# Parametric relu on ScalarE, and the mask added to the logits in PSUM by VectorE, in a two-layer graph attention kernel

## The chip, the cores and the metric

The program runs on one core of one Trainium2 chip. The metric is the device time of one execution in microseconds (us). The kernel before has a median of 1155.83 us over 3 runs (1154.28 to 1158.36).

## The reference

The input is x, 64 graphs of 128 nodes with 384 features, and adj, a boolean 128x128 matrix for each graph. Two layers follow each other, each with a residual and a layer norm:

```
# layer 0: six heads of 64
q, k, v = heads(x @ Wq + bq), heads(x @ Wk + bk), heads(x @ Wv + bv)
probs = softmax(q @ k.T / 8 + where(adj, 0, -9e15))
x1 = layernorm(x + (probs @ v) @ Wf + bf)

# layer 1: twelve heads of 32
h = x1 @ W1                       # per head
th = tanh(h)
attn = (th @ w_src) + (th @ w_dst).T
attn = where(attn >= 0, attn, 0.2 * attn)
attn = where(adj, attn, -999)
f = elu(softmax(attn) @ h + b1)
gate = sigmoid(x1 @ Hw.T + Hb)
out = layernorm(x1 + gate * f + (1 - gate) * x1)
```

## The kernel before, in words

All 64 graphs go through one software pipeline that is written out in full; every engine has its own list of instructions, and semaphores order them. The outer loop runs over groups g of four graphs, the inner loop over j = 0 to 3. In one iteration the kernel works on three graphs at once. TensorE also projects q, k and v of the next group (lines 267 to 322: in the iterations j = 0, 1 and 2 two projections with 512 columns each, in j = 3 the four projections of v). Graph ta = 4(g-1)+j is in its first layer's attention ("att" in the code). Graph tl = ta-2 is in the first half of the second layer ("gat"). The second layer's softmax, product and normalisation of tl-1 and tl-2 are the "tail". In the last group (graphs 60 to 63) there are no projections left, and after it two iterations have no first layer.

The order inside an iteration is fixed on each engine. On TensorE (lines 485 to 534): scores of ta, turn_f of tl-2, turn_x1 of tl, the first projection (fill_a), project_h, the second projection (fill_b), turn_p0, then the gate's product, the turns of the previous graph's weights (turn_p1), context and project_out in pieces, turn_sd, logits, the next scores' mask, apply_p1.

The second layer's logits are a sum of a row value and a column value for each head. Three bf16 parts of both lie in `sd3`; turn_sd transposes them into `ps_t` (a part of bank `ps_c`); ScalarE copies the row half into `rows_L` in three instructions (line 675), VectorE expands the column half into `cols_R` (line 891). A matmul of `rows_L` and `cols_R` then makes four heads' logits in one bank of `ps_d`; there are three banks, q = 0, 1, 2. Before it a matmul of a scaled identity (`ident_100`, 2^100) with `mask` (0 or -1, bf16) puts -2^100 where there is no edge (line 448). The leaky relu is made in two steps: ScalarE evicts Relu(0.8 x) to `z` (line 684), and VectorE computes z = 0.2 x + z (line 917). The next iteration takes the maxima of z (lines 805 and 813).

VectorE's order in the part touched is: `cols_R`; for the tail two graphs behind the second sum `r1` and its statistics (lines 897 to 901); the first layer's sum `r0` and its statistics (lines 908 to 912); the three steps of line 917. Then the next iteration begins with the maxima of the first layer's scores (line 783). ScalarE's first exponentials (line 615) wait for these, and `inv0` (line 811) for the exponentials.

GpSimd (lines 974 to 1012) takes, in each iteration: `p0` times `inv0` (line 982, which turn_p0 on TensorE waits for), `thw` (line 990), every now and then an addition for the residual or a split of x, then `normalise` for `r1` (it waits for `mv1_ready`, the end of line 901), and after that `normalise` for `r0` (it waits for `mv0_ready`, the end of line 912). Each `normalise` is four instructions (lines 967 to 972).

The first layer's mask comes from `ident_53` (2^53) times the same `mask`, in `scores_mask`.

Of the kernel before, what the change touches and what calls it, by code (L numbers as in the profile page):

```python
# [48 lines left out]
def build_program(nc, xT_in, x, adj, Wq, bq, Wk, bk, Wv, bv, Wf, bf, W1, b1, w_src, w_dst, HwT, Hb,  # L49
                  ident_in, pick_in, out):  # L50
    with ExitStack() as ctx:
        def sb(name, shape, dt=F32):
            return ctx.enter_context(nc.sbuf_tensor(name, shape, dt))
# [80 lines left out]
        def staging(buffer):  # L134
# [16 lines left out]
            sd_ready split_small sd3_ready sd_turned rows_ready cols_ready logits_ready relu_ready z_ready neg1_ready  # L151
# [34 lines left out]
        def has_tail(n, j, lag=1):  # L186
            return 0 <= G * (n - 1) + j - LAG - lag < B
# [62 lines left out]
        def _(pe):  # L250
# [84 lines left out]
            def scores_mask(t):  # L335

                if due(t):
                    pe.wait_ge(S["p0T_even"], t)
                    pe.wait_ge(S["p0T_odd"], t)
                if t % (B // 4) == 0:  # L340
                    pe.wait_ge(S["mask_ready"], t // (B // 4) + 1)
                if t == 0:
                    pe.wait_ge(S["consts_ready"], 3)
                    pe.wait_ge(S["bf_ready"], 1)
                for o in range(2):
                    pe.matmul(ps_s[:, o, 0:C * N].rearrange("p (i n) -> p i n", i=C), ident_53[:],  # L346
                              mask[:, t, :].unsqueeze(1).broadcast_to([P, C, N]), start=True, stop=False)

            def scores(g, par, j):
# [89 lines left out]
            def logits(t):  # L439

                pe.wait_ge(S["h_ready"], t + 1)
                pe.wait_ge(S["gate_ready"], t + 1)
                m = mask[:, t, :].unsqueeze(1) if isinstance(t, int) else mask[:, bass.ds(t, 1), :]
                for q in range(3):
                    if due(t):
                        pe.wait_ge(S[f"p1T_{q}"], t)
                    heads = ps_d[:, q, :].rearrange("p (a n) -> p a n", a=4)
                    pe.matmul(heads, ident_100[:], m.broadcast_to([P, 4, N]), start=True, stop=False)  # L448
                    if q == 0:
                        pe.wait_ge(S["rows_ready"], t + 1)  # L450
                        pe.wait_ge(S["cols_ready"], t + 1)
                    last = pe.matmul(heads, rows_L[:, q, :], cols_R[:], start=False, stop=True)  # L452
                    last.then_inc(S["logits_ready"], 1)

            def turn_p1(t, next_is_here, groups):
# [82 lines left out]
        def _(act):  # L538
# [25 lines left out]
            def iteration(g, par, n):  # L564
# [36 lines left out]
                for j in range(G):  # L601
# [68 lines left out]
                    if gat:  # L670
                        act.wait_ge(S["sd_turned"], tl + 1)
                        if due(tl):
                            act.wait_ge(S["logits_ready"], 3 * tl)
                        for q in range(3):
                            last = act.activation(rows_L[0:64, q, :], ps_t[0:64, :], ACT.Copy, scale=of_bank[0:64, q:q + 1])  # L675
                        last.then_inc(S["rows_ready"], 1)
                    if tail:
                        turned_p1(tl - 1, 2)
                    if gat:
                        for q in range(3):  # L680
                            act.wait_ge(S["logits_ready"], 3 * tl + q + 1)
                            if due(tl):
                                act.wait_ge(S["p1_turned"], 3 * (tl - 1) + q + 1)
                            act.activation(z[:, 4 * q:4 * q + 4, :], ps_d[:, q, :].rearrange("p (a n) -> p a n", a=4),  # L684
                                           ACT.Relu, scale=0.8).then_inc(S["relu_ready"], 1)
                    if tail:
                        act.wait_ge(S["ph_made"], tl)
                        if due(tl - 1):
# [7 lines left out]
        def _(dve):  # L696
# [19 lines left out]
            def small_constants():  # L716

                dve.wait_ge(S["ident_in_ready"], 16)
                dve.tensor_copy(ident_b[:], ident[:]).then_inc(S["consts_ready"], 1)
                dve.tensor_scalar(ident_53[:], ident[:], 2.0 ** 53, None, ALU.mult).then_inc(S["consts_ready"], 1)  # L720
                dve.tensor_scalar(ident_100[:], ident[:], 2.0 ** 100, None, ALU.mult).then_inc(S["consts_ready"], 1)
# [22 lines left out]
            def iteration(g, par, n):  # L744
# [29 lines left out]
                for j in range(G):  # L774
# [112 lines left out]
                    if gat:  # L887
                        dve.wait_ge(S["sd_turned"], tl + 1)
                        if due(tl):
# [1 line left out]
                        dve.tensor_tensor(cols_R[64:P, :, :], ps_t[64:P, :].unsqueeze(1).broadcast_to([64, 4, N]),  # L891
                                          of_slot[64:P, :].unsqueeze(2).broadcast_to([64, 4, N]), ALU.mult
                                          ).then_inc(S["cols_ready"], 1)
                    if has_tail(n, j, 2):
                        t2 = tl - 2
                        dve.wait_ge(S["tail_small"], 3 * t2 + 3)
                        dve.scalar_tensor_tensor(r1[:], r1[:], 0.25, x1_, ALU.mult, ALU.add).then_inc(S["r1_ready"], 1)
                        dve.wait_ge(S["r1_ready"], t2 + 1)
                        dve.bn_stats(st1, r1[:]).then_inc(S["mv1_ready"], 1)
                        dve.wait_ge(S["mv1_ready"], apart(dve, 2 * t2 + 1))  # L900
                        dve.bn_aggr(mv1, st1).then_inc(S["mv1_ready"], 1)  # L901
# [11 lines left out]
                    if gat:  # L913

                        for q in range(3):
                            dve.wait_ge(S["relu_ready"], 3 * tl + q + 1)
                            dve.scalar_tensor_tensor(z[:, 4 * q:4 * q + 4, :],  # L917
                                                     ps_d[:, q, :].rearrange("p (a n) -> p a n", a=4), 0.2,
                                                     z[:, 4 * q:4 * q + 4, :], ALU.mult, ALU.add
                                                     ).then_inc(S["z_ready"], 1)  # L920
            pipeline(dve, iteration)


        @block_.gpsimd
        def _(pool):
# [129 lines left out]
```

## Time and profile before

| | |
|---|---|
| median of 3 runs | 1155.83 us (1154.28 to 1158.36) |
| profiled execution, its own time | 1157.4 us |
| its span, first to last instruction | 1155.6 us |
| mean granted TensorE clock | 0.987 of full speed |
| TensorE matmul busy | 1093.0 us, 95% |
| VectorE busy | 989.8 us, 86% |
| ScalarE busy | 920.0 us, 80% |
| GpSimd busy | 544.0 us, 47% |

In the rows PE is TensorE's matmuls, PEld its weight loads, DVE VectorE, ACT ScalarE, POOL GpSimd, SP SyncE. L12 is line 12 of the kernel. Names such as `out<-in` are the program's buffers without their numbers. Matmuls overlap, so their busy time is more than the time between the starts. A busy share is an average over the whole span: it does not tell which engine another waits for.

### The profile page before, as it was taken

What the parts mean: (1) busy time and instruction counts of PE and PEld (TensorE: products, weight loads), DVE (VectorE), ACT (ScalarE), POOL (GpSimd) and SP (SyncE); (2) the same over time, 40 slices, a digit from 0 to 9 for tenths busy, and PEclk for the clock granted to TensorE, in tenths of its full rate; (3) what the DMA queues carried; (4) which work ended last, traced back from release to release, by engine and by line L of the source; (5) the groups of instructions that cost most, each with busy time, mean ns of one, the idle gap of its engine ahead of it and who ended that gap; (6) DMA issues with size and microseconds to landing.
All of it is one profiled execution on the core that took longest, in us unless ns stands there. A gap on an engine that the chain in (4) does not pass through costs nothing.

```text
span 1155.6 us, 25654 instructions
## 1 busy us (share of the span) xinstructions
PE 1093.0 (95%) x8364; PEld 900.8 (78%) x8428; DVE 989.8 (86%) x2022; ACT 920.0 (80%) x3383; POOL 544.0 (47%) x717
## 2 busy tenths in 40 slices
PE   5889999999999999999999999999999999997773
PEld 5668888888888888888888888888888888885652
DVE  5447989899898989889898998989898898989986
ACT  3338888888888888888888888888888888888875
POOL 0454544544454454445445444544544454444332
PEclk9989999999999999999999999999999999999997
DMA  9101010020101002010100101010010101000000
GB/s 264 55 2 55 16 48 34 10 70 16 62 15 52 32 9 69 16 62 15 52 31 9 70 15 63 16 51 34 8 69 15 63 15 43 15 8 15 15 14 21
DMA packets 25894, 44.67 MB, mean 39 GB/s; under 512 B 2462, under 2 KB 23714, under 8 KB 25762
## 3 DMA queue, kind: packets, MB, share of 16 engines
q1 hardware_dynamic: 23234, 41.91, 10.5%
q10 hardware_dynamic: 2496, 1.12, 0.5%
q8 instruction: 69, 1.13, 0.4%
q14 instruction: 63, 0.52, 0.1%
q0 software_dynamic: 32, 0.00, 0.0%
HBM read 30.43 MB, written 12.58 MB: 37 GB/s over the span
## 4 chain that ended last, share of the span: by engine, by line
PE 90%; DVE 3%; POOL 2%; issue 2%; ACT 2%; DMA 1%; POOLq 0%; ACTq 0%; DVEq 0%
PE ps_b L255 22%; PE ps_d L255 18%; PE ps_a L255 13%; PE ps_d L464 7%; PE ps_a L384 5%; PE ps_s L356 4%; PE ps_d L448 4%; PE ps_c L474 4%; PE ps_s L364 4%; PE ps_c L482 2%; PE ps_d L452 2%; PE ps_s L346 2%; PE ps_b L411 2%; ACT z L588 1%; PE ps_d L431 1%
## 5 line engine op out<-in xcount | busy, mean ns | idle before, releaser
L588 ACT ACTIVATE z<-z,s 128x128 f32<-128x128 f32 x768 | 299.2, 404 | 0.5 <-DVE s L805 0.5
L967 POOL TENSOR_SCALAR s<-s 128x1 f32<-128x1 f32 x128 | 28.6, 223 | 354.5 <-DVE s L901 325.7
L982 POOL TENSOR_TENSOR p<-p,s 128x768 f32<-128x768 f32 x64 | 94.2, 1472 | 181.2 <-DVE s L811 181.2
L615 ACT ACTIVATE p<-ps_s,s 128x128 f32<-128x128 f32 x384 | 135.4, 372 | 49.3 <-DVE s L783 49.3
L588 ACT ACTIVATION_READ_ACCUMULATOR z<-z,s 128x1 f32 x768 | 156.4, 204 | 0.0
L464 PE MATMUL ps_d<-ident,z 128*128 128x128 f32 x768 | 118.4, 277 | 9.4 <-ACT z L588 8.4
L990 POOL TENSOR_TENSOR thw<-th,w_sd 128x768 f32<-128x768 f32 x64 | 117.8, 1840 | 6.8 <-ACT th L638 6.8
L917 DVE SCALAR_TENSOR_TENSOR z<-ps_d,z 128x512 f32<-128x512 f32 x192 | 118.7, 674 | 0.9 <-ACT z L684 0.9
L684 ACT ACTIVATE z<-ps_d 128x512 f32<-128x512 f32 x192 | 100.8, 597 | 4.4 <-remote 0.5
L464 PEld LDWEIGHTS ps_d<-ident,z 128*128 128x128 f32 x768 | 90.6, 142 | 17.4 <-ACT z L588 9.2
L606 ACT ACTIVATE x1T_hi<-ps_b 128x384 fp32r<-128x384 f32 x64 | 31.6, 493 | 78.1 <-PE ps_b L411 78.1
L255 PE MATMUL ps_d<-hw_hi,x1T_hi 128*128 128x384 f32 x192 | 82.3, 429 | 0.0
L255 PE MATMUL ps_b<-wf_hi,ctxT_hi 128*128 128x384 f32 x192 | 79.2, 413 | 2.7 <-DVE ctxT_lo L749 1.3
L615 ACT ACTIVATION_READ_ACCUMULATOR p<-ps_s,s 128x1 f32 x384 | 80.6, 210 | 0.0
L448 PE MATMUL ps_d<-mask,ident 128*128 128x512 bf16 x192 | 73.5, 383 | 4.5 <-ACT rows_L L675 1.3
L805 DVE TENSOR_REDUCE s<-z 128x8 f32<-128x1024 f32 x64 | 77.3, 1208 | 0.0
L970 POOL TENSOR_TENSOR s<-s,minus_half 128x1 f32<-128x1 f32 x128 | 72.2, 564 | 10.7
L598 ACT ACTIVATE p1T<-ps_d 128x512 f32<-128x512 f32 x128 | 75.2, 588 | 0.7 <-PE ps_d L464 0.7
L836 DVE COPY p0T<-ps_s 128x384 f32<-128x384 f32 x64 | 35.7, 558 | 44.4 <-PE ps_s L364 44.2
L255 PE MATMUL ps_d<-w_hi,x1T_hi 128*128 128x384 f32 x192 | 65.2, 340 | 8.9 <-DVE x1T_lo L749 8.9
L255 PE MATMUL ps_b<-wf_lo,ctxT_hi 128*128 128x384 f32 x192 | 65.4, 340 | 0.0
L255 PE MATMUL ps_d<-hw_lo,x1T_hi 128*128 128x384 f32 x192 | 65.0, 338 | 0.0
(158 smaller groups left out, 3492.2 us busy)
## 6 DMA issues: line engine op xcount, KB each, us to landing
x_cols<-in_xT_dram SPq DMA_DIRECT2D x16, 768.0 KB, 6.2
xb<-in_x_dram SPq DMA_DIRECT2D x16, 768.0 KB, 4.7
out_dram<-y SPq DMA_DIRECT2D x64, 192.0 KB, 1.8
z<-in_L_gnn_Wq_dram SPq DMA_DIRECT2D x1, 576.0 KB, 7.0
p1T<-in_L_gnn_Wk_dram SPq DMA_DIRECT2D x1, 576.0 KB, 9.0
qT<-in_L_gnn_Wv_dram SPq DMA_DIRECT2D x1, 576.0 KB, 11.6
kT<-in_L_gnn_Wf_dram SPq DMA_DIRECT2D x1, 576.0 KB, 13.8
z<-in_L_gnn_W_dram SPq DMA_DIRECT2D x1, 576.0 KB, 11.5
```

The costliest lines, as they stand in the source:

```text
L255: last = pe.matmul(out_ap, lhs(a, c), rhs(b, c), start=(c == 0 and k == 0), stop=(closed and c == C - 1 and k == 2))
L448: pe.matmul(heads, ident_100[:], m.broadcast_to([P, 4, N]), start=True, stop=False)
L464: last = pe.transpose(ps_d[:, q, (a % 4) * N:(a % 4 + 1) * N], z[:, a, :], ident[:])
L588: done = act.activation(z[:, a, :], z[:, a, :], ACT.Exp, bias=neg1[:, a:a + 1], accum_out=sum1[:, a:a + 1])
L598: act.activation(p1T[:, 4 * q:4 * q + 4, :], ps_d[:, q, :].rearrange("p (a n) -> p a n", a=4), ACT.Copy).then_inc(S[f"p1T_{q}"], 1)
L615: last = act.activation(p0[:, o, i, :], ps_s[:, o, i * N:(i + 1) * N], ACT.Exp, bias=neg0[:, k:k + 1], accum_out=sum0[:, k:k + 1])
L684: act.activation(z[:, 4 * q:4 * q + 4, :], ps_d[:, q, :].rearrange("p (a n) -> p a n", a=4), ACT.Relu, scale=0.8).then_inc(S["relu_ready"], 1)
L805: dve.tensor_reduce(neg1[:, 0:8], z[:, 0:8, :], AX_X, ALU.max, negate=True).then_inc(S["neg1_ready"], 1)
L917: dve.scalar_tensor_tensor(z[:, 4 * q:4 * q + 4, :], ps_d[:, q, :].rearrange("p (a n) -> p a n", a=4), 0.2, z[:, 4 * q:4 * q + 4, :], ALU. ...
L970: pool.tensor_tensor(rs, ve, minus_half[:], ALU.pow).then_inc(S[small], 1)
L982: pool.tensor_tensor(p0[:].rearrange("p o i n -> p (o i) n"), p0[:].rearrange("p o i n -> p (o i) n"), inv0.unsqueeze(2).broadcast_to([P, ...
L990: pool.tensor_tensor(thw[:], th[:].unsqueeze(1).broadcast_to([P, 2, D]), w_sd[:], ALU.mult).then_inc(S["thw_ready"], 1)
```

## The change

The mask is scaled once, on GpSimd, to 0 or -2^53. The first layer adds it with the plain identity. In the second layer TensorE no longer adds it: the logits' matmul stands alone, and VectorE adds the mask to the bank in PSUM, in three instructions that stand directly behind `cols_R`. ScalarE then evicts the bank with a parametric relu (slope 0.2) straight to the finished `z`; VectorE's three steps of line 917 are gone. On VectorE the order behind the three additions is now: `r0` and its statistics, then `r1` and its statistics. GpSimd's order is as it was. `rows_ready` is counted once for each of the three copies instead of once for all.

```diff
@@ TensorE
-                    pe.matmul(ps_s[...], ident_53[:],
+                    pe.matmul(ps_s[...], ident_b[:],
                               mask[:, t, :]..., start=True, stop=False)
@@ logits
+                pe.wait_ge(S["cols_ready"], t + 1)
                 for q in range(3):
+                    pe.wait_ge(S["rows_ready"], 3 * t + q + 1)
                     if due(t):
                         pe.wait_ge(S[f"p1T_{q}"], t)
-                    pe.matmul(heads, ident_100[:], m.broadcast_to([P, 4, N]), start=True, stop=False)
-                    if q == 0:
-                        pe.wait_ge(S["rows_ready"], t + 1)
-                        pe.wait_ge(S["cols_ready"], t + 1)
-                    last = pe.matmul(heads, rows_L[:, q, :], cols_R[:], start=False, stop=True)
+                    last = pe.matmul(heads, rows_L[:, q, :], cols_R[:], start=True, stop=True)
                     last.then_inc(S["logits_ready"], 1)
@@ ScalarE
-                        last.then_inc(S["rows_ready"], 1)      # once for the three copies; now behind each
...
-                            act.wait_ge(S["logits_ready"], 3 * tl + q + 1)
+                            act.wait_ge(S["masked_ready"], 3 * tl + q + 1)
-                                           ACT.Relu, scale=0.8).then_inc(S["relu_ready"], 1)
+                                           ACT.Prelu, alpha=0.2).then_inc(S["z_ready"], 1)
@@ VectorE, constants
-                dve.tensor_scalar(ident_53[:], ident[:], 2.0 ** 53, None, ALU.mult)...
-                dve.tensor_scalar(ident_100[:], ident[:], 2.0 ** 100, None, ALU.mult)...
@@ VectorE, behind cols_R
-                    if has_tail(n, j, 2):          # r1 and its statistics: moved to the end
+                    if gat:
+                        for q in range(3):
+                            heads = ps_d[:, q, :].rearrange("p (a n) -> p a n", a=4)
+                            if tl % (B // 4) == 0:
+                                dve.wait_ge(S["mask_ready"], tl // (B // 4) + 1)
+                            dve.wait_ge(S["logits_ready"], 3 * tl + q + 1)
+                            dve.tensor_tensor(heads, heads, mask[:, tl, :]..., ALU.add
+                                              ).then_inc(S["masked_ready"], 1)
                     if att:                        # r0 and its statistics, as before
...
-                            dve.wait_ge(S["relu_ready"], 3 * tl + q + 1)
-                            dve.scalar_tensor_tensor(z[...], ps_d[...], 0.2, z[...], ALU.mult, ALU.add
-                                                     ).then_inc(S["z_ready"], 1)
+                    if has_tail(n, j, 2):          # r1 and its statistics, unchanged in themselves
@@ GpSimd
-                pool.tensor_scalar(mask[...], adj_u8[...], 1.0, -1.0, ALU.mult, ALU.add
+                pool.tensor_scalar(mask[...], adj_u8[...], 2.0 ** 53, -(2.0 ** 53), ALU.mult, ALU.add
```

## Rows read from the trace of the kernel before

**Rows 1.** The page, parts 1 and 4: busy time; shares of the last chain.
```profile
PE 1093.0 (95%) x8364; PEld 900.8 (78%) x8428; DVE 989.8 (86%) x2022; ACT 920.0 (80%) x3383; POOL 544.0 (47%) x717
...
PE 90%; DVE 3%; POOL 2%; issue 2%; ACT 2%; DMA 1%; POOLq 0%; ACTq 0%; DVEq 0%
```

**Rows 2.** Busy by stretch: from:to, length, PE, PEld, DVE, ACT, POOL, clock, DMA.
```profile
601.27:617.51 16.24, 16.19 (x128) 13.27 (x128) 15.07 (x31) 13.83 (x53) 8.40 (x11) 1.00 0.04 13
617.51:636.30 18.79, 18.65 (x147) 16.12 (x147) 15.48 (x32) 15.62 (x57) 10.21 (x12) 1.00 0.04 12
636.30:652.41 16.11, 16.06 (x127) 13.10 (x127) 15.06 (x31) 13.74 (x53) 6.62 (x10) 1.00 0.32 111
...
1088.03:1103.90 15.87, 12.51 (x110) 9.86 (x110) 14.35 (x31) 13.24 (x53) 6.61 (x10) 1.00 0.04 13
1103.90:1155.60 51.70, 27.53 (x212) 18.62 (x213) 37.20 (x75) 31.74 (x112) 13.68 (x26) 0.81 0.05 20
```

**Rows 3.** Waits over the span: who, for whom, us, times, longest.
```profile
POOL s L967 <- DVE s L901: 325.7, 64, 7.1
POOL p L982 <- DVE s L811: 181.2, 62, 4.3
```

**Rows 4.** Timeline of PE: start, us, what, idle before.
```profile
602.05 0.82 PE L448 MATMUL ps_d<-mask,ident 128*128 128x512 bf16 x2
602.71 0.38 PE L452 MATMUL ps_d<-cols_R,rows_L 128*128 128x512 bf16 x1
...
605.44 0.55 PE L482 MATMUL ps_c<-ident,fT 128*128 128x128 f32 x3
...
611.90 0.82 PE L364 MATMUL ps_s<-ident,p 128*128 128x128 f32 x6
...
624.21 0.41 PE L255 MATMUL ps_b<-wv_hi,xT_hi 128*128 128x384 f32 x1
```

**Rows 5.** Timeline of DVE.
```profile
601.27 0.69 DVE L891 TENSOR_TENSOR cols_R<-ps_c,choose 64x512 bf16<-64x512 bf16 x1 [0.15 <-PE ps_c L437]
602.00 0.56 DVE L897 SCALAR_TENSOR_TENSOR r<-r,x 128x384 f32<-128x384 f32 x1
...
603.40 0.56 DVE L908 TENSOR_TENSOR r<-ps_b,xb 128x384 f32<-128x384 f32 x1
...
604.69 1.85 DVE L917 SCALAR_TENSOR_TENSOR z<-ps_d,z 128x512 f32<-128x512 f32 x3
606.46 0.95 DVE L783 TENSOR_REDUCE s<-ps_s 128x6 f32<-128x768 f32 x1
...
623.56 0.55 DVE L749 TENSOR_TENSOR x1T_lo<-ps_b,x1T_hi 128x384 fp32r<-128x384 f32 x1
...
668.65 0.69 DVE L891 TENSOR_TENSOR cols_R<-ps_c,choose 64x512 bf16<-64x512 bf16 x1 [0.15 <-PE ps_c L437]
```

**Rows 6.** Timeline of POOL, the last row from the last group.
```profile
603.46 0.23 POOL L967 TENSOR_SCALAR s<-s 128x1 f32<-128x1 f32 x1 [4.63 <-DVE s L901]
...
606.76 0.67 POOL L972 TENSOR_SCALAR x<-r,s 128x384 f32<-128x384 f32 x1
609.96 1.47 POOL L982 TENSOR_TENSOR p<-p,s 128x768 f32<-128x768 f32 x1 [2.53 <-DVE s L811]
...
1096.71 1.47 POOL L982 TENSOR_TENSOR p<-p,s 128x768 f32<-128x768 f32 x1 [2.53 <-DVE s L811]
```

**Rows 7.** Timeline of ACT.
```profile
602.69 1.57 ACT L684 ACTIVATE z<-ps_d 128x512 f32<-128x512 f32 x3
604.70 0.49 ACT L690 ACTIVATE fT<-ps_c 128x384 f32<-128x384 f32 x1 [0.44 <-PE ps_c L474]
```

**Rows 8.** Groups by line, whole span: busy us, mean ns, idle before.
```profile
L917 DVE SCALAR_TENSOR_TENSOR z<-ps_d,z 128x512 f32<-128x512 f32 x192 | 118.7, 674 | 0.9 <-ACT z L684 0.9
...
L795 DVE TENSOR_TENSOR ps_c<-ps_c,s 128x384 f32<-128x384 f32 x64 | 36.2, 566 | 6.3 <-PE ps_c L482 4.2
...
L545 ACT ACT_TABLE_LOAD x1 | 1.3, 1283 | 0.9 <-issue 0.9
```

More of the change, by code:

```diff
@@ L70, in build_program @@
         ident_b = sb("ident_b", [P, P], BF16)
-        ident_53 = sb("ident_53", [P, P], BF16)
-        ident_100 = sb("ident_100", [P, P], BF16)
         choose = sb("choose", [P, 7])
@@ L150, in build_program @@
             x1_turned x1_hi x1_lo h_made h_ready th_ready gate_made gate_ready thw_ready
-            sd_ready split_small sd3_ready sd_turned rows_ready cols_ready logits_ready relu_ready z_ready neg1_ready
+            sd_ready split_small sd3_ready sd_turned rows_ready cols_ready logits_ready masked_ready z_ready neg1_ready
             exp1_ready p1_turned p1T_0 p1T_1 p1T_2 ph_made fT_ready f_turned inv1_ready f_ready minus_one_ready b1_ready
@@ L342, in scores_mask @@
                 if t == 0:
-                    pe.wait_ge(S["consts_ready"], 3)
+                    pe.wait_ge(S["consts_ready"], 1)
                     pe.wait_ge(S["bf_ready"], 1)
                 for o in range(2):
-                    pe.matmul(ps_s[:, o, 0:C * N].rearrange("p (i n) -> p i n", i=C), ident_53[:],
+                    pe.matmul(ps_s[:, o, 0:C * N].rearrange("p (i n) -> p i n", i=C), ident_b[:],
                               mask[:, t, :].unsqueeze(1).broadcast_to([P, C, N]), start=True, stop=False)
@@ L442, in logits @@
                 pe.wait_ge(S["gate_ready"], t + 1)
-                m = mask[:, t, :].unsqueeze(1) if isinstance(t, int) else mask[:, bass.ds(t, 1), :]
+                pe.wait_ge(S["cols_ready"], t + 1)
                 for q in range(3):
+                    pe.wait_ge(S["rows_ready"], 3 * t + q + 1)
                     if due(t):
@@ L674, in iteration @@
                         for q in range(3):
-                            last = act.activation(rows_L[0:64, q, :], ps_t[0:64, :], ACT.Copy, scale=of_bank[0:64, q:q + 1])
-                        last.then_inc(S["rows_ready"], 1)
+                            act.activation(rows_L[0:64, q, :], ps_t[0:64, :], ACT.Copy, scale=of_bank[0:64, q:q + 1]
+                                           ).then_inc(S["rows_ready"], 1)
                     if tail:
@@ L719, in small_constants @@
                 dve.tensor_copy(ident_b[:], ident[:]).then_inc(S["consts_ready"], 1)
-                dve.tensor_scalar(ident_53[:], ident[:], 2.0 ** 53, None, ALU.mult).then_inc(S["consts_ready"], 1)
-                dve.tensor_scalar(ident_100[:], ident[:], 2.0 ** 100, None, ALU.mult).then_inc(S["consts_ready"], 1)
                 dve.wait_ge(S["const_in"], 16 * 7)
@@ L893, in iteration @@
                                           ).then_inc(S["cols_ready"], 1)
-                    if has_tail(n, j, 2):
[L895 to L901, printed above, removed]
+                    if gat:
[4 more added lines that the diff above has]
+                            dve.wait_ge(S["logits_ready"], 3 * tl + q + 1)
+                            dve.tensor_tensor(heads, heads, mask[:, tl, :].unsqueeze(1).broadcast_to([P, 4, N]), ALU.add
+                                              ).then_inc(S["masked_ready"], 1)
                     if att:
@@ L912, in iteration @@
                         dve.bn_aggr(mv0, st0).then_inc(S["mv0_ready"], 1)
-                    if gat:
-                        for q in range(3):
-                            dve.wait_ge(S["relu_ready"], 3 * tl + q + 1)
-                            dve.scalar_tensor_tensor(z[:, 4 * q:4 * q + 4, :],
-                                                     ps_d[:, q, :].rearrange("p (a n) -> p a n", a=4), 0.2,
-                                                     z[:, 4 * q:4 * q + 4, :], ALU.mult, ALU.add
-                                                     ).then_inc(S["z_ready"], 1)
+                    if has_tail(n, j, 2):
+                        t2 = tl - 2
+                        dve.wait_ge(S["tail_small"], 3 * t2 + 3)
+                        dve.scalar_tensor_tensor(r1[:], r1[:], 0.25, x1_, ALU.mult, ALU.add).then_inc(S["r1_ready"], 1)
+                        dve.wait_ge(S["r1_ready"], t2 + 1)
+                        dve.bn_stats(st1, r1[:]).then_inc(S["mv1_ready"], 1)
+                        dve.wait_ge(S["mv1_ready"], apart(dve, 2 * t2 + 1))
+                        dve.bn_aggr(mv1, st1).then_inc(S["mv1_ready"], 1)
             pipeline(dve, iteration)
@@ L942, in mask_quarter @@
                 pool.wait_ge(S["adj_in"], 16)
-                pool.tensor_scalar(mask[:, quarter, :], adj_u8[:, quarter, :], 1.0, -1.0, ALU.mult, ALU.add
+                pool.tensor_scalar(mask[:, quarter, :], adj_u8[:, quarter, :], 2.0 ** 53, -(2.0 ** 53), ALU.mult, ALU.add
                                    ).then_inc(S["mask_ready"], 1)
```

## The prediction

> **What bounds the kernel now.** I read the page first. TensorE is busy for 95% of the span and holds 90% of the chain that ended last; VectorE has 86%, GpSimd 47% [rows 1]. By this page TensorE is the bound, and a change that takes matmuls from it should pay. The second view was the stretches, cut at the starts of `cols_R` (L891), since the changed work stands right behind it. An iteration takes 16.24 us (j = 2, and j = 1 is the same within 0.01), 18.79 us (j = 3) or 16.11 us (j = 0) [rows 2]. A group of four takes 668.65 - 601.27 = 67.38 us [rows 5]. In these stretches TensorE has no idle time to speak of. But the row 1088.03:1103.90 speaks against the page. It is from the last group, where TensorE has no projections left and is busy for 12.51 us only, and the iteration still takes 15.87 us [rows 2]. So there is a second loop, only 0.24 to 0.37 us shorter than TensorE's. Taking more than that from TensorE brings nothing in j = 0, 1, 2, and whatever lengthens the second loop by more than that shows in the time.
>
> The second loop is found with the waits and the timelines. GpSimd waits 181.2 us in 62 waits for `inv0` (L811) [rows 3]. In the last group `p0` times `inv0` (L982) starts 1096.71 - 1088.03 = 8.68 us behind `cols_R`, and the next `cols_R` follows 1103.90 - 1096.71 = 7.19 us later [rows 2, 6]. In the full stretch it starts 609.96 - 601.27 = 8.69 us behind, the same, and ends at 611.43; TensorE comes to turn_p0 at 611.90, 0.47 us later [rows 4 to 6]. So the loop is: `cols_R`, the rest of VectorE's list, the maxima (L783), ScalarE's six exponentials, `inv0`, `p0` on GpSimd, turn_p0, and from there work that the change leaves alone up to the next `cols_R`.
>
> The other wait of GpSimd, 325.7 us for L901 [rows 3], looks harmless, since it is idle time of an idle engine. It tells that GpSimd takes `r1` first, in program order, and that its two normalisations are set off by the end of VectorE's `r1`. They run from 603.46 to 606.76 + 0.67 = 607.43, 3.97 us together, and leave 2.53 us before `inv0` comes [rows 6].
>
> **The change part by part.** Times below are counted from the start of `cols_R` (601.27).
>
> TensorE: three mask matmuls go. From 602.05 to 602.71 it issues three of these 512-column matmuls, 0.22 us each [rows 4], so 0.66 us an iteration. As a matmul with the same columns, the first layer's mask costs what it did, since only its constant changes.
>
> VectorE, the work: three steps of L917 go (674 ns, three of them advance VectorE from 604.69 to 606.46, 1.77 us) [rows 5, 8], and three additions of the same 512 columns come, PSUM to PSUM with a bf16 operand. The trace has no such instruction at this size. Its nearest rows are L917 from below (674 ns) and, from above, L795, in place in PSUM with 384 columns (566 ns), to which 128 columns at about 1.05 ns make some 700 ns [rows 8]. The additions are thus worth 0 to 0.1 us more in sum; I take 0, so 1.77 us.
>
> VectorE, the new wait: the first addition needs the first bank's logits, which need `cols_R`. `cols_R` ends at +0.69, TensorE is free for the logits at 602.05, +0.78, and such a matmul takes 0.38 us [rows 4, 5]; with a hand-over the addition starts at +1.20. Before, VectorE went on at 602.00, +0.73, with `r1` [rows 5]. So 0.47 us of idle time is new. Bounds: 0.35 if the matmul is seen sooner, 0.6 if TensorE has to wake up for it. Queued behind it on VectorE are `r0`, `r1` and the maxima L783. The third bank's matmul also waits for ScalarE's last copy of p1T, just ahead of 602.69, and is there before the third addition at about +2.4.
>
> VectorE, the new order: additions +1.20 to +2.97; the `r0` part as between 603.40 and 604.69, 1.29 us, to +4.26; the `r1` part as between 602.00 and 603.40, 1.40 us, to +5.66; then L783. It started at 606.46, +5.19, before [rows 5]. L783 is 0.47 us late.
>
> GpSimd: this is where the order bites. It starts on `r1` 603.46 - 602.00 = 1.46 us after VectorE's first `r1` instruction [rows 5, 6], now at 4.26 + 1.46 = +5.72 instead of +2.19. Both normalisations need 3.97 us, so GpSimd is free at +9.7; with a gap between two of its instructions I take +9.75. `inv0`, 0.47 us late, would have let `p0` start at 8.69 + 0.47 = +9.16. So `p0` starts at +9.75, 1.06 us late, and 0.59 us of that is GpSimd's queue. Bounds: 9.65 and 9.95.
>
> From `p0` to the next `cols_R` it is 7.19 us, measured in the group where TensorE has idle time [rows 2, 6]. The new iteration is 9.75 + 7.19 = 16.94 us: +0.70 against 16.24, +0.83 against 16.11, +1.07 in the last group against 15.87. TensorE's 0.66 us are gone into waiting for `p0`.
>
> In j = 3 TensorE has over 2 us more of projections and GpSimd's queue is covered: `p0` has over a microsecond of room there. But project_v(1) at 624.21 waits for x1T_lo, which follows L783 on VectorE (623.56 + 0.55 = 624.11) [rows 4, 5]. It is 0.47 us late, and behind it TensorE is busy without a gap up to turn_p0. So j = 3 costs +0.47. The 0.66 us saved ahead of it do not help, because turn_f (605.44) now waits for `fT`.
>
> ScalarE: the count of instructions stays. A Prelu of the same tile with immediate scale is put at Relu's 597 ns; three take 1.57 us from first start to last end [rows 7]. They follow the additions: the third ends near +3.07, its Prelu near +3.7, `fT` (0.49 us) near +4.15; TensorE can start turn_f at about +4.2. It starts at 605.44, +4.17, now [rows 4, 7]. No loss, no gain.
>
> Start and end: two small constants less on VectorE, worth 0.3 us at most, and one late L749 after graph 63, 0.5 us. Both together +0.2. `rows_ready` counted singly is hidden by `cols_R`, which the first logits wait for anyway. No DMA is touched.
>
> **The sum.** `r1` exists from graph 4 on, so the new order reaches `p0` of graphs 5 to 63. Groups of graphs 4 to 59, 14 of them: 0.83 + 0.70 + 0.70 + 0.47 = 2.70 us each, 37.8, less 0.8 for graph 4. Last group: 4 x 1.07 = 4.3. With 0.2 for start and end: +41.5 us. The profiled execution, 1157.4 us with a span of 1155.6, would take 1198.9. It lay 1.6 us above the median 1155.83, so I say 1197.5 us, 3.6% slower. With the bounds of `p0`'s start (9.65 to 9.95) and of the additions the sum is +34 to +55.
>
> **A page's rule against the price of Prelu.** The trace has one ACT_TABLE_LOAD, of 1283 ns, for all of Copy, Identity, Exp, Tanh and Relu [rows 8]. The Trainium skill, page "ScalarE: Activation LUTs", section "Table sets: the hidden batching unit", says that cheap functions are filler in every set and names relu, copy, identity and abs, but not the parametric relu; a function of another set is preceded by a load. It puts a switch, drain included, at about 2.66 us; by that, two switches in each of 64 iterations would be an estimated 340 us and the time about 1540.
>
> **The rivals.**
> A. GpSimd's queue does not bind, because its normalisations run closer together or `inv0` comes later than I think. Then only VectorE's wait counts: `p0` at +9.16, the iteration 16.35 us, +0.11, +0.11, +0.24 and +0.47 in a group, 14 x 0.93 + 4 x 0.48 = 15 us: 1171. For it: the 2.53 us of idle time before L982 [rows 6]. Against it: L967 moves by 3.53 us, more than that room and the 0.47 us together (3.00).
> B. The other side: TensorE is the bound, as the page says, and VectorE catches up. Then the saving is limited by the last group's loop: 0.37 + 0.37 + 0.24 in j = 1, 2, 0 and 0.66 in j = 3, 1.64 us in a group, 15 groups: -25 us, 1131. It decides if `p0` starts at or before 16.24 - 7.19 = +9.05, so if the additions wait for nothing and GpSimd is not held. For it: 90% of the last chain is PE [rows 1]. Against it: every step of the walk.
> C. Prelu isn't in the table in use. Two loads of 1283 ns in each of 64 iterations, 164 us if nothing covers them; ScalarE waits 0.44 us before `fT` [rows 7] and for the maxima, so perhaps half is seen: 1280, from 1230 to 1360.
> D. The granted clock falls, since TensorE gets idle time. Against it: it is 1.00 in the last group with TensorE busy for 12.51 of 15.87 us, and 0.81 only in the drained end [rows 2]. No case of its own.
>
> **How the numbers follow.** Forecast 0.82 (1189 to 1210), A 0.07, B 0.04, C 0.04, and 0.03 for a wash of unknown parts near 1156. A measurement of this kernel can tell 0.3%, some 3.5 us, from no change. Faster 0.04, the same 0.03, slower 0.93. The range runs from 1174, towards A, to 1210, the upper bounds.
>
> **What would show it.** In the changed trace: `cols_R` to `cols_R` about 16.9 us in j = 0, 1, 2 and 19.3 in j = 3, and the last group also 16.9, no longer shorter than the rest. Idle time of about 0.5 us on VectorE ahead of the first addition. L982 no longer waiting 2.5 us for VectorE but starting right behind L972. TensorE idle for `p0` ahead of L364 by over 1 us in most iterations. Additions of 670 to 700 ns, Prelu near 600 ns, one table load. I am wrong if L982 still waits for `inv0`, or if iterations of j = 0, 1, 2 are under 16.3 us.

## The result and the profile after

The changed kernel takes 1210.51 us (median of 4 runs, 1208.89 to 1211.59), the kernel before, in the same sessions, 1157.09. The ratio is 1.046, with a 95% interval of 1.0444 to 1.0477. The forecast was 1197.5 us, 3.6% slower: the sign and the two mechanisms (VectorE's new wait and GpSimd's queue) were right, and the time lies 0.5 us above the range. The rise is 53.4 us where about 42 was forecast, so a fifth of it was missed; 1.3 us of the distance to 1197.5 is only the starting point, which was the earlier median of 1155.83. The profiled execution has a span of 1209.8 us, 54.2 us more than before.

First the page of the changed kernel, parts 1 and 4. TensorE's share of the last chain has gone from 90% to 52%, GpSimd's from 2% to 19%, VectorE's from 3% to 21% [rows 1].

```profile
PE 1103.7 (91%) x8236; PEld 882.5 (73%) x8236; DVE 989.7 (82%) x2020; ACT 927.3 (77%) x3383; POOL 542.4 (45%) x717
...
PE 52%; DVE 21%; POOL 19%; issue 6%; ACT 2%; DMA 0%; POOLq 0%; ACTq 0%; DVEq 0%
```

The stretches, cut at the starts of `cols_R` as in [rows 2]: a j = 1 iteration, j = 3, j = 0, one of the last group, one of the drained end (the two iterations that follow it and have no first layer).

```profile
608.70:625.78 17.08, 16.42 (x126) 12.81 (x125) 15.06 (x31) 13.93 (x53) 8.37 (x11) 1.00 0.04 13
642.87:662.33 19.46, 18.41 (x145) 15.84 (x144) 15.47 (x32) 15.71 (x57) 10.22 (x12) 1.00 0.04 12
662.33:679.44 17.11, 16.24 (x125) 12.68 (x124) 15.06 (x32) 13.86 (x54) 6.58 (x10) 1.00 0.31 105
1120.58:1137.67 17.09, 13.51 (x108) 10.63 (x107) 14.34 (x30) 13.39 (x52) 6.57 (x10) 0.90 0.04 13
1169.17:1185.12 15.95, 10.24 (x63) 7.72 (x61) 11.36 (x24) 9.57 (x36) 3.49 (x5) 0.81 0.04 14
```

Every iteration but j = 3 now takes 17.1 us, with TensorE's projections or without. That is what a bound away from TensorE looks like. (j = 2, 625.78 to 642.87, takes 17.09 us.) The first four of these rows show the iterations that the sum was about; the last one matters for the size of the miss.

The waits of the changed kernel. GpSimd waited for `inv0` 62 times before [rows 3]; now it does 17 times, in j = 3 and at the start. In the others it comes late to an `inv0` that is already there, and TensorE waits for it.

```profile
POOL s L960 <- DVE s L913: 542.7, 64, 10.9
...
DVE ps_d L893 <- PE ps_d L447: 41.3, 64, 1.3
...
PEld ps_s L362 <- POOL p L975: 36.6, 46, 2.0
...
POOL p L975 <- DVE s L804: 19.1, 17, 1.6
```

The timeline of VectorE from one `cols_R` (591.60) to the next (608.70): the wait for the logits, the three additions, r0, r1, the maxima.

```profile
591.60 0.69 DVE L884 TENSOR_TENSOR cols_R<-ps_c,choose 64x512 bf16<-64x512 bf16 x1
592.92 1.90 DVE L893 TENSOR_TENSOR ps_d<-ps_d,mask 128x512 f32<-128x512 f32 x3 [0.63 <-PE ps_d L447]
594.84 0.56 DVE L901 TENSOR_TENSOR r<-ps_b,xb 128x384 f32<-128x384 f32 x1
...
596.13 0.53 DVE L909 SCALAR_TENSOR_TENSOR r<-r,x 128x384 f32<-128x384 f32 x1
...
597.38 0.94 DVE L776 TENSOR_REDUCE s<-ps_s 128x6 f32<-128x768 f32 x1
...
608.70 0.69 DVE L884 TENSOR_TENSOR cols_R<-ps_c,choose 64x512 bf16<-64x512 bf16 x1 [0.16 <-PE ps_c L435]
```

The timeline of GpSimd in the same iteration. `p0` (L975) follows r0's normalisation without a gap, where 2.53 us of idle time stood [rows 6].

```profile
597.55 0.23 POOL L960 TENSOR_SCALAR s<-s 128x1 f32<-128x1 f32 x1 [7.48 <-DVE s L913]
...
600.86 0.67 POOL L965 TENSOR_SCALAR x<-r,s 128x384 f32<-128x384 f32 x1
601.49 1.48 POOL L975 TENSOR_TENSOR p<-p,s 128x768 f32<-128x768 f32 x1
```

The timeline of TensorE there: the logits, turn_f waiting for `fT`, the first of project_h, turn_p0 waiting for `p0`. The wait for `p0` is short here (0.27 us), because TensorE has already lost time at the logits, at `fT` and at x1T_lo; in the last group, from which the last row is, it is 1.07 us.

```profile
592.50 0.88 PE L447 MATMUL ps_d<-cols_R,rows_L 128*128 128x512 bf16 x3
...
595.88 0.55 PE L477 MATMUL ps_c<-ident,fT 128*128 128x128 f32 x3 [0.51 <-ACT fT L685]
...
598.84 0.44 PE L253 MATMUL ps_d<-w_hi,x1T_hi 128*128 128x384 f32 x1
...
603.02 0.88 PE L362 MATMUL ps_s<-ident,p 128*128 128x128 f32 x6 [0.27 <-POOL p L975]
...
1132.00 0.87 PE L362 MATMUL ps_s<-ident,p 128*128 128x128 f32 x6 [1.07 <-POOL p L975]
```

The groups of the changed instructions: the addition, Prelu, the one table load.

```profile
L893 DVE TENSOR_TENSOR ps_d<-ps_d,mask 128x512 f32<-128x512 f32 x192 | 121.3, 693 | 41.3 <-PE ps_d L447 41.3
...
L679 ACT ACTIVATE z<-ps_d 128x512 f32<-128x512 f32 x192 | 114.6, 598 | 47.6 <-DVE ps_d L893 47.5
...
L540 ACT ACT_TABLE_LOAD x1 | 1.3, 1283 | 1.0 <-issue 1.0
```

### The profile page after: what moved, and what is told of

The parts are those of the page before. It is cut to its first block, busy times and chain, and to the rows that moved or that the text cites. A ratio compares the mean times of both kernels' runs of the same rounds, so it can differ in the third digit from the quotient of the medians.

```text
span 1209.8 us, 25470 instructions
## 1 busy us (share of the span) xinstructions
PE 1103.7 (91%) x8236; PEld 882.5 (73%) x8236; DVE 989.7 (82%) x2020; ACT 927.3 (77%) x3383; POOL 542.4 (45%) x717
## 4 chain that ended last, share of the span: by engine, by line
PE 52%; DVE 21%; POOL 19%; issue 6%; ACT 2%; DMA 0%; POOLq 0%; ACTq 0%; DVEq 0%
PE ps_b L253 14%; PE ps_d L253 12%; DVE ps_d L893 10%; PE ps_d L459 7%; PE ps_a L253 5%; POOL p L975 5%; POOL s L963 4%; PE ps_s L362 4%; PE ps_a L382 4%; POOL x L965 3%; POOL y L965 3%; DVE r L901 2%; DVE s L911 2%; DVE s L903 2%; PE ps_d L447 2%
## 5 line engine op out<-in xcount | busy, mean ns | idle before, releaser
L893 DVE TENSOR_TENSOR ps_d<-ps_d,mask 128x512 f32<-128x512 f32 x192 | 121.3, 693 | 41.3 <-PE ps_d L447 41.3
L679 ACT ACTIVATE z<-ps_d 128x512 f32<-128x512 f32 x192 | 114.6, 598 | 47.6 <-DVE ps_d L893 47.5
L975 POOL TENSOR_TENSOR p<-p,s 128x768 f32<-128x768 f32 x64 | 94.3, 1473 | 19.1 <-DVE s L804 19.1
L253 PE MATMUL ps_d<-w_hi,x1T_hi 128*128 128x384 f32 x192 | 71.9, 374 | 11.0 <-DVE x1T_lo L742 10.7
L362 PE MATMUL ps_s<-ident,p 128*128 128x128 f32 x384 | 54.9, 279 | 16.2 <-POOL p L975 16.2
L362 PEld LDWEIGHTS ps_s<-ident,p 128*128 128x128 f32 x384 | 42.2, 140 | 37.5 <-POOL p L975 36.6
L253 PE MATMUL ps_d<-w_hi,x1T_lo 128*128 128x384 f32 x192 | 67.3, 350 | 0.0
```

Of the source, the lines that this page charges most:

```text
L253: last = pe.matmul(out_ap, lhs(a, c), rhs(b, c), start=(c == 0 and k == 0), stop=(closed and c == C - 1 and k == 2))
L362: last = pe.transpose(ps_s[:, o, i * N:(i + 1) * N], p0[:, o, i, :], ident[:])
L893: dve.tensor_tensor(heads, heads, mask[:, tl, :].unsqueeze(1).broadcast_to([P, 4, N]), ALU.add).then_inc(S["masked_ready"], 1)
L975: pool.tensor_tensor(p0[:].rearrange("p o i n -> p (o i) n"), p0[:].rearrange("p o i n -> p (o i) n"), inv0.unsqueeze(2).broadcast_to([P, ...
```

## The experiments

"Iteration" below is the time from `cols_R` to `cols_R` in j = 1 and 2 of the full stretch (the iterations in which TensorE projects); offsets count from `cols_R`'s start. The diffs give the order of the lists in words; apart from what they say the instructions are unchanged. Kernels before in the same sessions: 1158.68, 1156.24 and 1157.64 us.

| run | iteration / j = 3, us | median, us | ratio (95%) |
|---|---|---|---|
| before | 16.24 / 18.78 | 1157 | 1 |
| the change | 17.09 / 19.4 | 1210.5 | 1.046 (1.0444 to 1.0477) |
| GpSimd r0 first | 16.64 / 19.4 | 1192.5 | 1.029 (1.0266 to 1.0315) |
| r1 ahead of r0 | 16.90 / 19.4 | 1204.2 | 1.040 (1.038 to 1.0416) |
| GpSimd r0 first, fT early | 16.62 / 19.4 | 1189.7 | 1.028 (1.0247 to 1.0306) |
| wait filled | 16.37 / 18.65 | 1169.8 | 1.011 (1.0079 to 1.0135) |
| wait filled, GpSimd r0 first | 16.35 / 18.65 | 1165.8 | 1.007 (1.005 to 1.0095) |
| the same, fT early | 15.91 / 18.65 | 1145.1 | 0.990 (0.9887 to 0.992) |
| additions last | 20.0 / 22.2 | 1368.2 | 1.183 (1.1799 to 1.1864) |
| before, r1 last | 16.63 / 18.9 | 1177.7 | 1.018 (1.0145 to 1.0208) |
| before, Prelu alone | 16.24 / 18.45 | 1151.1 | 0.994 (0.9917 to 0.9957) |
| two banks by TensorE | 16.03 / 18.23 | 1136.5 | 0.983 (0.9817 to 0.9846) |
| one bank by TensorE | 15.80 / 18.50 | 1135.2 | 0.982 (0.9806 to 0.9836) |
| one bank, two ahead of v | 15.79 / 18.23 | 1128.1 | 0.975 (0.9722 to 0.9779) |

**The order of the sums alone, in the kernel before.**

```diff
-  cols_R; r1 part; r0 part; three steps of the leaky relu
+  cols_R; r0 part; three steps of the leaky relu; r1 part
```

> The kernel before with one thing of the change only: VectorE's r1 part stands last, behind r0 and the three steps of the leaky relu. VectorE has the same work and no new wait. Theory: GpSimd starts at 3.79 + 1.46 = +5.25 instead of +2.19, is free at +9.2, p0 starts there instead of +8.69, the iteration is 9.2 + 7.19 = 16.35 to 16.4 us in j = 0, 1, 2 (16.24, 16.24, 16.11 before) and in the last group (15.87), j = 3 as before: about +8 us, 1165. Rival (the order of the sums costs nothing by itself): 1157 us.

Measured: 1177.7 us, 19 us more than before, with the same work on every engine; 8 us was expected. The mechanism held and its size was larger: r0, now first, waits 0.28 us for TensorE (`out_made`), which I had not counted, and `p0` starts at 617.29 - 607.87 = +9.42, not +9.2. The next `cols_R` follows 7.21 us later. GpSimd in this run:

```profile
613.35 0.23 POOL L967 TENSOR_SCALAR s<-s 128x1 f32<-128x1 f32 x1 [7.62 <-DVE s L920]
...
616.66 0.67 POOL L972 TENSOR_SCALAR x<-r,s 128x384 f32<-128x384 f32 x1
617.29 1.47 POOL L982 TENSOR_TENSOR p<-p,s 128x768 f32<-128x768 f32 x1
```

**GpSimd's order repaired in the changed kernel.**

```diff
-  normalise(r1 ...); normalise(r0 ...)
+  normalise(r0 ...); normalise(r1 ...)
```

> The changed kernel with GpSimd normalising r0 first and r1 second, VectorE as it is. Theory: r0's normalisation can start at +4.6, r1's follows at +6.6 and ends near +8.6, before inv0; p0 waits for inv0 again and starts at +9.3 instead of +9.89, so an iteration of j = 0, 1, 2 takes 16.5 us instead of 17.09, j = 3 stays at 19.4, the last group 16.5; about 1182 us in all. L982's counterpart waits for VectorE's inv0 again in all iterations. Rival (the additions' wait alone): no change, 1210 us.

Measured: 1192.5 us and 16.64 us an iteration. A third of the 53 us was GpSimd's order (in the iterations of j = 1 and 2 it is 0.45 of 0.85 us), since `p0` waits for `inv0` again and starts at 623.59 - 614.32 = +9.27, as expected. But 9.27 + 7.19 would make 16.46. The rest is on TensorE: project_h starts 0.05 us after x1T_lo (620.96 + 0.55 = 621.51 on VectorE), at +7.24 instead of 608.24 - 601.27 = +6.97 in the kernel before, and TensorE is busy from there through turn_p0, which it reaches after `p0` is ready (625.06). The last group gained nothing: `p0` starts at 1111.47 - 1102.20 = +9.27 there too, but the granted clock is 0.90 and the iteration 17.10 us instead of the 16.5 expected. GpSimd's row, VectorE's, TensorE's, and TensorE's in the kernel before:

```profile
623.59 1.47 POOL L975 TENSOR_TENSOR p<-p,s 128x768 f32<-128x768 f32 x1 [0.38 <-DVE s L804]
```
```profile
620.96 0.55 DVE L742 TENSOR_TENSOR x1T_lo<-ps_b,x1T_hi 128x384 fp32r<-128x384 f32 x1
```
```profile
621.56 0.45 PE L253 MATMUL ps_d<-w_hi,x1T_hi 128*128 128x384 f32 x1
...
625.34 0.82 PE L362 MATMUL ps_s<-ident,p 128*128 128x128 f32 x6
```
```profile
608.24 0.33 PE L255 MATMUL ps_d<-w_hi,x1T_hi 128*128 128x384 f32 x1
```

**VectorE's order repaired instead.**

```diff
-  three additions; r0 part; r1 part
+  three additions; r1 part; r0 part
```

> The changed kernel with VectorE's r1 part ahead of the r0 part, both still behind the three additions. Theory (GpSimd's queue is what delays p0): its normalisations start at about +4.7 (first r1 instruction +3.24, plus 1.46) instead of +5.95 and no longer hold p0, which would go at +9.3. But r0 now ends at about +5.2 instead of +3.8, and turn_x1 on TensorE waits for it (it started at +4.66), with 6.1 us of TensorE work from there to turn_p0: so a new wait takes the place of the old one, the iteration is 16.9 to 17.0 us instead of 17.09 and the whole about 1203 us. Rival (only GpSimd's queue counts): 16.5 us an iteration, about 1183 us. Rival (the additions' own work and wait is all, the order of the sums costs nothing): no change, 1210 us.

Measured: 1204.2 us, 16.90. The expectation of a new wait held: turn_x1 on TensorE now waits for r0. Its row:

```profile
627.60 0.55 PE L409 MATMUL ps_b<-ident,x 128*128 128x128 f32 x3 [0.33 <-DVE r L909]
```

**GpSimd r0 first, and `fT` early.** ScalarE takes `fT` behind the first Prelu.

```diff
-  Prelu 0, Prelu 1, Prelu 2, fT
+  Prelu 0, fT, Prelu 1, Prelu 2
```

> The changed kernel with GpSimd normalising r0 first (as in the run before with that alone, 16.64 us) and, besides, ScalarE taking fT behind the first Prelu, so that turn_f on TensorE waits for nothing (it idles 0.4 us there). Theory: nothing is gained, 1192 us and 16.64 us, because project_h still waits for x1T_lo at +7.2, which follows the late maxima on VectorE. Rival (the late fT is what costs 0.4 us an iteration): 16.25 us, 1167.

Measured: 1189.7 us and 16.62 us: the wait for `fT` (0.4 us) is gone and has moved to project_h, as expected.

```profile
620.35 0.44 PE L253 MATMUL ps_d<-w_hi,x1T_hi 128*128 128x384 f32 x1 [0.51 <-DVE x1T_lo L750]
```

**The wait filled.** r1's first instruction stands in VectorE's wait for the logits.

```diff
-  cols_R; three additions; r0 part; r1 part
+  cols_R; r1 sum; three additions; r0 part; r1 statistics
```

> The changed kernel with one thing moved: r1's first instruction stands between cols_R and the three additions, in VectorE's wait for the logits. GpSimd keeps its order. Theory: the maxima come at +5.1 instead of +5.8, GpSimd starts on r1 at +5.25 instead of +5.95, frees p0 at +9.1 to 9.2: 16.3 to 16.4 us an iteration instead of 17.09, j = 3 18.8, about 1165 us. Rival (the additions' work costs, not the wait): less than 0.2 us an iteration gained, over 1200 us.

Measured: 1169.8 us, 16.37. One instruction of 0.56 us moved into the wait takes 41 us off. The maxima start at 608.37 - 603.32 = +5.05 although the additions are all still there. The total is 5 us above the expected one, the iteration as expected. In the last group of the profiled execution two iterations take 16.37 us and two 17.9 us, with the same instructions; the granted clock is 0.81 in the longer ones. VectorE, then two of these iterations:

```profile
608.37 0.94 DVE L776 TENSOR_REDUCE s<-ps_s 128x6 f32<-128x768 f32 x1
```
```profile
1061.49:1079.40 17.91, 14.43 (x107) 11.48 (x107) 14.25 (x31) 13.65 (x53) 6.56 (x10) 0.81 0.03 12
1079.40:1095.77 16.37, 12.06 (x107) 9.54 (x107) 14.24 (x30) 13.36 (x52) 6.57 (x10) 1.00 0.04 14
```

**The wait filled, and GpSimd r0 first.** Both edits together.

```diff
-  cols_R; three additions; r0 part; r1 part            # VectorE
-  normalise(r1 ...); normalise(r0 ...)                 # GpSimd
+  cols_R; r1 sum; three additions; r0 part; r1 statistics
+  normalise(r0 ...); normalise(r1 ...)
```

> As the run with the wait filled alone, and GpSimd normalising r0 first as well. Theory: p0 goes at +8.6 and the iteration is TensorE's again with turn_f 0.1 us later than in the kernel before: 16.35 us, j = 3 18.7, about 1157 us; what is missing against the version that also takes fT early (15.91 us, 1145) is the wait for fT. Rival (GpSimd's queue no longer matters once the wait is filled): the same as the wait filled alone.

Measured: 1165.8 us, 16.35. The iteration is as expected, the total 9 us above. In the full stretch the rival was right: with the wait filled, `p0` behind GpSimd's queue (+9.16, here +8.55) is no later than TensorE with its late turn_f, so repairing the queue brings 0.02 us an iteration. That is 1 us of the 4 us between the two runs. In the profiled executions they differ in the last group and the drained end, where this run has no iteration at a clock of 0.81; how much of the rest is the queue and how much the clock was not separated.

**The same, and `fT` early on ScalarE.**

```diff
-  Prelu 0, Prelu 1, Prelu 2, fT
+  Prelu 0, fT, Prelu 1, Prelu 2
```

> The changed kernel with all three additions on VectorE, and three things moved: r1's first instruction stands between cols_R and the additions (in the wait for the logits), GpSimd normalises r0 first, ScalarE takes fT behind the first Prelu. Theory: L783 at +5.35 instead of +5.78, p0 at +8.85 and no longer behind GpSimd's queue, turn_f not held by fT; iteration 16.05 us in j = 0, 1, 2, 18.95 in j = 3, 16.03 in the last group, about 1155 us: what the change costs is gone, but hardly anything is gained. Rival (the additions cost by themselves, whatever stands where): still over 1185 us.

Measured: 1145.1 us, 15.91; better than expected, since the maxima come at +5.06 and not +5.35. Here the change's whole content is kept and it is 1.0% faster than the kernel before. The rival falls: the three additions by themselves do not cost the loss. VectorE of this run has no idle time between `cols_R` and r0:

```profile
591.79 0.69 DVE L892 TENSOR_TENSOR cols_R<-ps_c,choose 64x512 bf16<-64x512 bf16 x1 [0.16 <-PE ps_c L435]
592.52 0.56 DVE L898 SCALAR_TENSOR_TENSOR r<-r,x 128x384 f32<-128x384 f32 x1
593.11 1.90 DVE L905 TENSOR_TENSOR ps_d<-ps_d,mask 128x512 f32<-128x512 f32 x3
594.92 0.55 DVE L913 TENSOR_TENSOR r<-ps_b,xb 128x384 f32<-128x384 f32 x1
```

**The additions where the old steps stood.**

```diff
-  three additions; r0 part; r1 part
+  r1 part; r0 part; three additions
```

> The changed kernel with VectorE's order as in the kernel before: r1, r0, and the three additions last, where the three steps of the leaky relu stood. Theory: the maxima L783 come at +5.35 (5.19 before), GpSimd is as before, so neither of the two delays of the changed kernel is there; but ScalarE's three Prelus now follow additions that end at +4.2, +4.8 and +5.4, fT starts near +6.0 instead of +3.4, and turn_f stands ahead of turn_x1 and the projections on TensorE: turn_f at +6.5 instead of +4.17, so TensorE loses about 2.3 us an iteration, 18.5 us instead of 16.24, and the whole goes to about 1290 us. Rival (ScalarE has time: it waited 1.15 us ahead of L606): an iteration of 16.3 us, 1160 us.

Measured: 1368.2 us, 20.0 us an iteration. turn_f starts at 750.02 - 743.68 = +6.34, close to the +6.5 expected; 1.5 us an iteration more than the expected 18.5 is there besides. It is the granted clock: 0.91 over the stretch, and behind the idle time of 2.58 us the next 512-column matmuls start 0.43 to 0.57 us apart instead of 0.23. The trace has its own comparison. Five iterations of its full stretch ran at 1.00, and those of j = 0, 1, 2 among them took 18.42 us, with the same wait for `fT`: TensorE idles 2.49 us in both the second and the third row below (j = 1 and j = 2 of one group). The stretch from 743.68, these two, then TensorE in the first:

```profile
743.68:763.41 19.73, 17.06 (x125) 13.99 (x124) 15.11 (x31) 13.95 (x53) 6.65 (x10) 0.91 0.27 91
438.10:458.08 19.98, 17.49 (x126) 14.18 (x125) 15.10 (x31) 14.05 (x53) 8.43 (x11) 0.91 0.03 11
458.08:476.50 18.42, 15.93 (x126) 12.97 (x125) 15.11 (x31) 13.93 (x53) 8.40 (x11) 1.00 0.03 12
```
```profile
750.02 0.90 PE L477 MATMUL ps_c<-ident,fT 128*128 128x128 f32 x3 [2.58 <-ACT fT L685]
...
751.22 0.78 PE L253 MATMUL ps_a<-xT_hi,wq_hi 128*128 128x512 f32 x1
751.79 0.63 PE L253 MATMUL ps_a<-xT_hi,wq_lo 128*128 128x512 f32 x1
```

**Prelu alone, in the kernel before.**

```diff
-  ScalarE: Relu(0.8 x) -> z;  VectorE: z = 0.2 x + z
+  ScalarE: Prelu(x, 0.2) -> z
```

> The kernel before with the parametric relu alone: TensorE still adds the mask, ScalarE evicts with Prelu straight to z, VectorE's three steps of the leaky relu are gone (1.77 us an iteration) and nothing takes their place. Theory: TensorE is the bound in the full stretch and has all its work, so j = 0, 1, 2 stay at 16.24, 16.24, 16.11 although VectorE gets 1.77 us; j = 3 loses 0.25 us (project_v(1) waits for x1T_lo no longer); the last group goes from 15.87 to about 15 us. About -8 us, 1149. Rival (VectorE's work is the bound): 1.8 us an iteration less than 16.24 where nothing else holds, up to 60 us less, 1100.

Measured: 1151.1 us, 16.24 unchanged, j = 3 18.45. Taking 1.77 us an iteration from an engine that is busy 86% of the time brought 0.6%. Nothing of it is in j = 0, 1, 2; it is in j = 3, where project_v(1) waited for x1T_lo, and in the last group (15.40 us instead of 15.88; 15 was expected).

**The mask shared between the engines.** TensorE masks the first bank or banks (identity times mask ahead of the logits), VectorE adds it to the others; VectorE's order is r1, r0, additions; `fT` behind the Prelus that need no addition.

```diff
+  if q < by_pe: pe.matmul(heads, ident_b[:], mask..., start=True, stop=False)
-  for q in range(3): add mask     # VectorE, ahead of r0 and r1
+  for q in range(by_pe, 3): add mask     # VectorE, behind r1 and r0
```

> A version meant to keep the gain: Prelu; TensorE masks bank 0 in its product (the identity times the mask), VectorE adds the mask to banks 1 and 2 only; VectorE's order r1, r0, additions; ScalarE takes fT behind the first Prelu, ahead of the other two. Theory: TensorE saves 0.44 us an iteration, VectorE 0.5 us (1.77 against two additions), L783 at about +4.8, p0 at +8.3, GpSimd not held; TensorE is the bound at 15.8 to 15.9 us in j = 0, 1, 2, j = 3 about 18.5, last group 15.5: about 1137 us. Rival (a late x1T_hi behind the last Prelu at +5.4 makes up for it): 16.2 us, 1155.

> As the version with one bank masked by TensorE, but with banks 0 and 1 masked by TensorE and bank 2 alone by VectorE. Theory: TensorE saves 0.22 us an iteration, VectorE 1.1 us; TensorE is the bound at 16.02, 16.02, 15.9 us, j = 3 about 18.3 (x1T_lo is early), the last group about 15.0: about 1138 us. Rival (VectorE, not TensorE, is what bounds): clearly faster than the version with one bank, by the 0.6 us an iteration that VectorE has less, 1100 us.

Measured: 1135.2 and 1136.5 us, 15.80 and 16.03 us. Both are TensorE's old times less 0.44 and 0.22 us, two and one of its matmuls. In j = 0, 1, 2 VectorE's work does not show, so the rival falls. In j = 3 it does: the version with more work on TensorE and less on VectorE takes 18.23 us there, the other 18.50, which is what the next run uses.

**One bank by TensorE, two ahead of the v projections.**

```diff
-  by_pe = 1
+  by_pe = 2 if j == 2 else 1
```

> The version with one bank masked by TensorE, but in the iteration ahead of the four v projections (j = 2) TensorE masks two banks, so that VectorE is earlier at x1T_lo, which project_v(1) waits for. Theory: 15.80, 15.80, 15.71 us stay and j = 3 falls from 18.50 to 18.22 us, what the version with two banks had there; 4 us less, 1131 us. Rival (j = 3 is bound by TensorE's work alone): the added matmul of 0.22 us makes it slower, 1138.

Measured: 1128.1 us (expected 1131), j = 3 18.23 us. It beats both kernels: 2.5% under the one before, 6.8% under the changed one. TensorE's busy time fills its stretches again:

```profile
586.64:602.42 15.78, 15.73 (x126) 12.96 (x126) 14.51 (x31) 13.82 (x54) 8.42 (x11) 1.00 0.04 14
602.42:620.65 18.23, 18.18 (x146) 15.98 (x146) 14.45 (x31) 15.65 (x57) 10.22 (x12) 1.00 0.04 12
```

## Why the prediction was right in kind and too small

The mechanism was right; three terms of the sum were too small. The start of `p0` was taken as +9.75 us and was +9.89, so an iteration took 17.09 us and not 16.94. The term of j = 3 was taken as +0.47 and was +0.6. Start and end were taken as +0.2 and were +3.6. By the starts of `cols_R` in the two profiled executions the rise of 54.2 us divides as follows: +0.3 up to the `cols_R` ahead of graph 5's `p0` (113.53 against 113.25), +45.7 from there to the last group (at 1086.38 against 1040.38; forecast 37.8 - 0.8 = 37.0), +4.9 in the last group (forecast 4.3), +3.3 in the drained end and what follows it. Of the 12.7 us that were missed, 9.3 are in the iterations and 3.4 in start and end.

- **The second loop.** Right. `p0` to the next `cols_R` was taken as 7.19 us; in the changed kernel it is 608.70 - 601.49 = 7.21.
- **The additions, the Prelu, the table.** Right. 693 ns against 674 to 700, 598 against 597, one table load. Rival C falls. The Trainium skill, "ScalarE: Activation LUTs", section "Table sets: the hidden batching unit", has cheap functions in every set without naming this one. By the one load of 1283 ns Prelu is among those that need no switch here, and none of the estimated 340 us is there.
- **VectorE's new wait: too small.** Forecast +1.20 for the first addition; it is +1.32 here and +1.38 in other iterations (644.25 - 642.87). TensorE was at the logits at +0.78 by its work, but its first one starts at 592.50 - 591.60 = +0.90: once it has to wait for `cols_R`, the matmul starts 0.21 us after that ends. The idle time that is new was taken as 0.47 us, with an upper bound of 0.6; it is 0.63 (592.92 less the end of `cols_R` at 592.29).
- **The hand from the additions to r0: too small.** 594.84 - 592.92 = 1.92 us where the old steps gave 1.77. Of the 0.15 us between them 0.05 is the longer additions (1.90 against 1.85) and 0.10 the hand: r0's sum starts 0.02 us after the third addition has ended, whereas L783 began 0.08 us before the old steps' end. r1 was 0.15 us cheaper than taken (1.25 against 1.40), but it stands behind r0, so GpSimd's start saw 1.92 + 1.29 + 1.42 = 4.63 us behind the first addition. I had 4.52. Together with the later first addition GpSimd starts at +5.95 instead of +5.72.
- **GpSimd's queue: right in kind, 0.14 us too early.** From its start to `p0` it needs 601.49 - 597.55 = 3.94 us, 0.09 less than taken, so `p0` starts at +9.89 against +9.75, within its bounds of 9.65 and 9.95. This makes the iteration 17.09 instead of 16.94, and with j = 3 a group of four 3.3 us longer instead of 2.7.
- **The sign on TensorE failed.** It was to idle for `p0` by over 1 us in most iterations. It does so in the last group (1.07 us) but not in the full stretch (0.27 us), where it first waits for `cols_R`, for `fT` (0.51 us) and for x1T_lo.
- **j = 3: right path, +0.6 instead of +0.47.** The first addition starts at 644.25 - 642.87 = +1.38, and project_v(1) at 650.22 - 642.87 = +7.35, where it was 624.21 - 617.51 = +6.70. The slower hand and the shorter r1 cancel here, since both stand ahead of x1T_lo.
- **Start and end: the term that was furthest off for its size.** Forecast +0.2; measured +3.6. The stretch behind the last group grew from 51.70 [rows 2] to 1209.80 - 1154.76 = 55.04 us. Of that, 0.5 us is in the first drained iteration, 2.15 in the second and 0.7 behind it. The two iterations in the changed kernel, then in the kernel before:

```profile
1154.76:1169.17 14.41, 8.97 (x72) 6.49 (x70) 12.43 (x26) 10.77 (x39) 5.14 (x9) 1.00 0.04 14
1169.17:1185.12 15.95, 10.24 (x63) 7.72 (x61) 11.36 (x24) 9.57 (x36) 3.49 (x5) 0.81 0.04 14
```
```profile
1103.90:1117.80 13.90, 9.91 (x70) 7.07 (x69) 12.35 (x26) 9.70 (x37) 5.16 (x9) 0.91 0.04 14
1117.80:1131.60 13.80, 8.70 (x67) 6.22 (x68) 11.36 (x23) 10.79 (x39) 3.50 (x5) 0.97 0.04 16
```

  In the second one project_h starts at 1175.67 - 1169.17 = +6.50 against 1124.18 - 1117.80 = +6.38, so only 0.12 us is lost up to there. Its nine matmuls then start 0.32 us apart instead of 0.17, and the rest is lost from there on. I had dismissed rival D by the last group alone, and the drained end was where the clock could fall. (In the last group it is 0.90 now, and the iteration is 17.09 us all the same, since `p0` sets it.) This is one execution of each kernel. No run separated the clock's part of the 3.3 us from that of the changed order, so this stays open.
- **Missed path.** x1T_lo holds project_h in every iteration, not only project_v(1) in j = 3. Rival A's 16.35 us should have been 16.64, as the run with GpSimd's order repaired shows. It changed nothing in the sum, because `p0` was later still. Rival A falls all the same: `p0` follows r0's normalisation without a gap, and `inv0` had been ready.
- **Rival B** falls: with everything in place the change's own form gives 15.91 us, but not in this order.

## What to carry to other kernels

A chain of waits that is 90% TensorE does not say how far the next loop is behind. Look for a stretch in which TensorE has less work: if the period barely falls (here from 16.24 to 15.87 us), the difference is all that can be gained from TensorE, and all the delay that the other loop can take before it shows. When two results feed a queue on another engine in program order, moving the first behind the second delays both; check each consumer's order before moving a producer. A new wait is cheap if an independent instruction of its length can stand in it, and work moved off the bound engine is best moved in the share that the receiving engine has room for.

## What the runs showed of the hardware that I had not expected

With about 2.5 us without a matmul in each iteration (additions last) TensorE's granted clock was 0.91 or 0.92 in 50 of the 55 iterations from graph 5 to the last group and 1.00 in the other five, though the wait was the same: 19.98 us against 18.42. In the last group waits of 1.61 and 1.69 us in one iteration left it at 1.00 in the kernel before, and waits of 2.09 and 1.07 us went with 0.90 in the changed one. Idle times of 0.3 to 0.5 us in the full stretch went with 1.00. So the clock of a stretch has to be read in its row and cannot be told from one wait. An in-place addition in PSUM (fp32 bank, bf16 operand repeated four times, 512 columns) took 693 ns, 19 ns more than the leaky relu's step from PSUM to SBUF (674 ns).
